# Cross-attention in a six-part decoder block: transposed scores on two 64-row groups, with the queries kept twice, in place of 17 rows on 32-row groups

## The reference, cut to what matters

```python
def _L0_xattn_ref(query, key, values, mask, W_out):
    q = query.reshape(N, Q, HEADS, HEAD_DIM)
    k = key.reshape(N, K, HEADS, HEAD_DIM)
    v = values.reshape(N, K, HEADS, HEAD_DIM)
    energy = jnp.einsum('nqhd,nkhd->nhqk', q, k)
    energy = jnp.where(mask == 0, jnp.float32(-1e+20), energy)
    attn = jax.nn.softmax(energy / jnp.sqrt(jnp.float32(EMB)), axis=-1)
    out = jnp.einsum('nhqk,nkhd->nqhd', attn, v).reshape(N, Q, EMB)
    return out @ W_out.T
...
    x = x + _L0_attn_ref(_layernorm(x, axis=-1), L0_attn_Wq, ...)
    x = x + _L0_xattn_ref(_layernorm(x, axis=-1), ctx_1024, ctx_1024, mask_Bx1x1xS2_ik0, L0_xattn_W_out)
    x = x + _L0_ffn_ref(_layernorm(x, axis=-1), ...)
    x = x + _L1_attn_ref(_layernorm(x, axis=-1), ...)
    x = x + _L1_xattn_ref(_layernorm(x, axis=-1), ctx_1024, ctx_1024, ...)
    x = x + _L1_ffn_ref(_layernorm(x, axis=-1), ...)
```

## Time and profile before

| | |
|---|---|
| median of 3 runs | 1816.44 us (1815.75 to 1816.7) |
| the profiled execution | 1815.63 us |
| its span, first to last instruction | 1813.8 us |
| PE busy | 1689.0 us (93%) |
| DVE, ACT, POOL busy | 777.8, 634.3, 441.8 us |
| mean granted TensorE clock | 0.846 of full speed |
| the chain that ended last | PE 85%, DVE 7% |
| L641 in that chain | 10% of the span |

### The profile page before, as it was taken

The page is one execution under the profiler, slowest core; times in us unless marked ns, Lnnn a source line. Parts: engine busy times, 40 slices in busy tenths (PEclk is TensorE's granted clock), DMA queues, the critical chain, the costliest instruction groups (busy, mean ns, idle before and its releaser), DMA issues.

```text
span 1813.8 us, 32813 instructions
## 1 busy us (share of the span) xinstructions
PE 1689.0 (93%) x11795; PEld 1158.1 (64%) x11795; DVE 777.8 (43%) x1752; ACT 634.3 (35%) x1684; POOL 441.8 (24%) x519
## 2 busy tenths in 40 slices
PE   5999999989999999987999799999998999699995
PEld 5888888757766766753555447565666666465653
DVE  4555555443333333314555412111204565456665
ACT  1221112112222223224666541312214666254552
POOL 2000000011101101008888410000003333345551
PEclk8999999955555555558999899999998999899996
DMA  6300000001110111040000010000000000000001
GB/s 181 54 1 0 0 0 0 1 19 28 36 37 19 36 37 27 1 153 1 1 0 0 1 44 0 1 0 0 0 0 6 1 0 1 6 9 10 8 6 41
DMA packets 33034, 34.72 MB, mean 19 GB/s; under 512 B 8913, under 2 KB 29633, under 8 KB 32945
## 3 DMA queue, kind: packets, MB, share of 16 engines
q1 hardware_dynamic: 32944, 33.48, 7.3%
HBM read 31.49 MB, written 1.86 MB: 18 GB/s over the span
## 4 chain that ended last, share of the span: by engine, by line
PE 85%; DVE 7%; issue 2%; ACT 2%; POOL 2%; DMA 1%; SPq 1%; DVEq 0%; ACTq 0%; POOLq 0%
PE banks L276 40%; PE banks L641 10%; PE banks L680 6%; PE banks L628 6%; PE banks L269 4%; PE banks L657 4%; PE banks L548 3%; PE banks L693 3%; PE banks L706 2%; PE banks L520 2%; PE banks L683 1%; DVE area L1427 1%; DMA room<-in_bo 1%; PE banks L869 1%; PE banks L715 1%
## 5 line engine op out<-in xcount | busy, mean ns | idle before, releaser
L1131 ACT ACTIVATE area<-banks,area 112x112 f32<-112x112 f32 x768 | 208.5, 360 | 147.0 <-DVE area L1427 135.4
L1395 DVE TENSOR_REDUCE Y_room<-banks 112x2 f32<-112x750 f32 x128 | 115.4, 936 | 244.3 <-PE banks L628 244.3
L680 PE MATMUL banks<-area 128*112 128x448 f32 x384 | 180.1, 551 | 6.9 <-POOL area L964 3.6
L1110 ACT ACTIVATE area<-banks,Y_room 125x896 f32<-125x896 f32 x96 | 96.7, 1007 | 231.1 <-PE banks L641 231.1
L269 PE MATMUL banks<-cst,area 112*128 112x112 f32 x576 | 102.0, 295 | 71.8 <-DVE area L1470 21.6
L1427 DVE TENSOR_REDUCE area<-banks 112x4 f32<-112x448 f32 x192 | 119.2, 621 | 93.0 <-PE banks L683 92.6
L255 POOL TENSOR_TENSOR rstd<-mv,kcol 112x1 f32<-112x1 f32 x80 | 15.2, 190 | 554.6 <-DVE mv L1265 515.2
L269 PEld LDWEIGHTS banks<-cst,area 112*128 112x128 f32 x576 | 64.2, 152 | 115.3 <-issue 83.9
L276 PE MATMUL banks<-area,room 128*128 128x112 f32 x1024 | 125.0, 286 | 5.8 <-DVE area L1292 3.6
L276 PEld LDWEIGHTS banks<-area,room 128*128 128x128 f32 x1024 | 122.9, 202 | 6.3 <-DVE area L1292 3.8
L693 PEld LDWEIGHTS banks<-cst,area 112*112 112x112 f32 x768 | 87.5, 133 | 55.6 <-issue 44.1
(11 more groups left out here) (214 smaller groups left out, 2905.3 us busy)
## 6 DMA issues: line engine op xcount, KB each, us to landing
Y_room<-in_ctx SPq DMA_DIRECT2D x16, 375.0 KB
area<-in_ctxT SPq DMA_DIRECT2D x64, 93.8 KB
l<-in_l SPq DMA_DIRECT2D x2, 1024.0 KB, 10.4
room<-in_ctxT SPq DMA_DIRECT2D x16, 112.0 KB, 2.1
out<-X SPq DMA_DIRECT2D x16, 112.0 KB, 1.9
X<-in_x SPq DMA_DIRECT2D x1, 1568.0 KB, 20.7
room<-in_Wq SPq DMA_DIRECT2D x1, 1024.0 KB, 7.6
room<-in_Wk SPq DMA_DIRECT2D x1, 1024.0 KB, 9.8
```

Of the source, the lines that this page charges most:

```text
L680: T3.matmul(pb[2 + g % 2][0:S, 0:4 * S], c_qT[u][:, k, :], c_kbd[u][:, k, j:j + 4, :].rearrange("p j s -> p (j s)"), start=True, stop=False)
L1110: a_.activation(b_pT[g][:, c, :, :], banks[0:KC, 4:6, 0:QN], ACT.Exp, bias=b_bias[v][:, c:c + 1]).then_inc(Bs["ex"].sem, 1)
L1131: last = a_.activation(c_p[:, h * S:(h + 1) * S], pb[2 + g % 2][0:S, j * S:(j + 1) * S], ACT.Exp, bias=c_nb[:, h:h + 1])
L1395: v_.tensor_reduce(b_nb[u][:, 8 * a + k:8 * a + k + 5:4], banks[0:S, 2 * a:2 * a + 2, 0:SC], AX_X, ALU.max, negate=True).then_inc(Bs["nb"] ...
```

## The change

`turned` contracts over 64 rows, two slots together, in place of 17 rows of one slot. Which head of the pair is meant is said by the queries: `b_q` is now kept twice (g = 0 and 1), and copy g has the rows of the other slot of each half zeroed. ACT makes the two copies from the same transposed bank, each with a column of scales that is 1/16 on one slot of each half and 0 on the other (a new constant, `C_HALF`). So that the two heads e that go together lie in different halves of the array, the heads' slots are ordered anew: slot r holds a = r % 2, c = r // 2, in `b_ctx`, in `b_xs` and in the columns of `b_nb`.

The mask row now lies within the 64 rows and has to be zero for `turned`. So `b_nb` has 32 columns, 16 of them zero (two memsets on POOL in the first stage), its transpose has 32 rows, and SP writes them with four DMAs: for each copy g the maxima into row 16 of its slots and zeros into row 17. `scores_b` still contracts over 18 rows of each slot, from the copy in which the slot is live. All four buffers of `b_q` move to `room`, where the first stage's weights were.

```diff
-C_END = C_LT + 16
+C_HALF = C_LT + 16
+C_END = C_HALF + 2
...
+    c[:, C_HALF:C_HALF + 2] = ((p[:, None] // SLOT) % 2 == np.arange(2)[None, :]) * D ** -0.5
...
-        b_q = [take(P, QN) for _ in range(2)]
+        b_q = [room[:, 2 * i * QN:2 * (i + 1) * QN].rearrange("p (g n) -> p g n", g=2) for i in range(4)]
...
-        b_nb, b_rc, b_nt = [beside_y(S, H) for _ in range(2)], beside_y(S, H), beside_y(H, S)
-        b_q = [beside_y(P, QN) for _ in range(2)] + b_q
+        b_nb, b_rc, b_nt = [beside_y(S, 2 * H) for _ in range(2)], beside_y(S, H), beside_y(2 * H, S)
...
-                    src = T["ctxT"][bass.ds(b, 1)].rearrange("o (a k c i) s -> a c (o i) k s", a=2, k=QUAD, c=2)[r // 2, r % 2]
+                    src = T["ctxT"][bass.ds(b, 1)].rearrange("o (a k c i) s -> a c (o i) k s", a=2, k=QUAD, c=2)[r % 2, r // 2]
...
-                    sp.dma_start(b_q[(w - 1) % 4][HD:P:SLOT, :].rearrange("r (k s) -> r k s", k=QUAD),
-                                 b_nt).then_inc(Bs["mr"].sem, 16)
+                    for n in range(4):
+                        first = SLOT * (n // 2) + HD + n % 2
+                        sp.dma_start(b_q[(w - 1) % 4][first:P:2 * SLOT, n // 2, :].rearrange("e (k s) -> e k s", k=QUAD),
+                                     b_nt[8 * n:8 * (n + 1), :]).then_inc(Bs["mr"].sem, 16)
...
-                    T3.transpose(pb[7][0:H, 0:S], b_nb[(w - 1) % 2], ident[0:S, 0:S]).then_inc(Bs["mt"].sem, 1)
+                    T3.transpose(pb[7][0:2 * H, 0:S], b_nb[(w - 1) % 2], ident[0:S, 0:S]).then_inc(Bs["mt"].sem, 1)
...
-                    last = T3.matmul(pb[r][0:S, 0:SC], b_q[w][o:o + HD + 2, k * S:(k + 1) * S], b_ctx[w][o:o + HD + 2, k, 0:SC],
+                    last = T3.matmul(pb[r][0:S, 0:SC], b_q[w][o:o + HD + 2, r % 2, k * S:(k + 1) * S], b_ctx[w][o:o + HD + 2, k, 0:SC],
...
-                        o = SLOT * (2 * g + e)
-                        last = T3.matmul(pb[4 + e][0:KC, k * S:(k + 1) * S], b_ctx[w][o:o + HD + 1, k, c * KC:(c + 1) * KC],
-                                         b_q[w][o:o + HD + 1, k * S:(k + 1) * S], start=True, stop=True)
+                        o = 2 * SLOT * e
+                        last = T3.matmul(pb[4 + e][0:KC, k * S:(k + 1) * S], b_ctx[w][o:o + 2 * SLOT, k, c * KC:(c + 1) * KC],
+                                         b_q[w][o:o + 2 * SLOT, g, k * S:(k + 1) * S], start=True, stop=True)
...
-                    a_.activation(b_q[(w + 1) % 4], pb[7][:, 0:QN], ACT.Copy, scale=D ** -0.5).then_inc(Bs["qs"].sem, 1)
+                    for g in range(2):
+                        last = a_.activation(b_q[(w + 1) % 4][:, g, :], pb[7][:, 0:QN], ACT.Copy,
+                                             scale=cst[:, C_HALF + g:C_HALF + g + 1])
+                    last.then_inc(Bs["qs"].sem, 1)
```

More of the change, by code:

```diff
@@ L635, in turned @@
                 if n == 0:
-                    pe.wait_ge(Bs["mr"].sem, Bs["mr"].at(16 * (b + 1)))
+                    pe.wait_ge(Bs["mr"].sem, Bs["mr"].at(64 * (b + 1)))
                 pe.wait_ge(Bs["ex"].sem, Bs["ex"].at(6 * b + n))
@@ L944, in phase_a @@
                     g_.memset(b_cv[1][:, :, :, HD:HD + 1], 1.0)
+                    for t in b_nb:
+                        g_.memset(t, 0.0)
                     g_.memset(b_xs[:, :], 0.0).then_inc(pre["bx"].sem, 1)
@@ L1076, in phase_b @@
                     act.wait_ge(Bs["mt"].sem, Bs["mt"].at(b))
-                    act.wait_ge(Bs["mr"].sem, Bs["mr"].at(16 * (b - 1)))
-                    a_.activation(b_nt, pb[7][0:H, 0:S], ACT.Copy).then_inc(Bs["me"].sem, 1)
+                    act.wait_ge(Bs["mr"].sem, Bs["mr"].at(64 * (b - 1)))
+                    a_.activation(b_nt, pb[7][0:2 * H, 0:S], ACT.Copy).then_inc(Bs["me"].sem, 1)
                 if on(b - 2):
@@ L1370, in phase_b @@
                     for a in range(2):
-                        dst = b_xs.rearrange("s (k a c e) -> s a k c e", k=QUAD, a=2, c=2)[:, a, :, :, 0:HD]
+                        dst = b_xs.rearrange("s (k c a e) -> s a k c e", k=QUAD, a=2, c=2)[:, a, :, :, 0:HD]
                         src = xb_(b + 1, a * P, (a + 1) * P).rearrange("s (k c e) -> s k c e", k=QUAD, c=2)
@@ L1394, in highest @@
                     dve.wait_ge(Bs["mt"].sem, Bs["mt"].at(b - 1))
-                v_.tensor_reduce(b_nb[u][:, 8 * a + k:8 * a + k + 5:4], banks[0:S, 2 * a:2 * a + 2, 0:SC], AX_X, ALU.max,
+                v_.tensor_reduce(b_nb[u][:, 4 * a + k:4 * a + k + H + 1:H], banks[0:S, 2 * a:2 * a + 2, 0:SC], AX_X, ALU.max,
                                  negate=True).then_inc(Bs["nb"].sem, 1)
```

## The result

The kernel takes **1653.2 us** with the change, the median of four runs (1651.6 to 1660.9), against 1816.3 before (1815.8 to 1816.7). The ratio is 0.911 (95% interval 0.909 to 0.913): 163 us less, where the forecast was 173 and its range 1612 to 1710.

A forecast was written before the change was run, and what follows sets the result against it. PE bound all stages, cross-attention at 1.2 GHz. A batch of 13.3 + 0.2 + 0.45 + 1.05 = 15.0 us, taken as 15.1 for 26.65, over 15.0 batches saves 173: 1816.4 - 173 = 1643 us; range 1612 to 1710.

The forecast's parts named there:

- The clock decides, and rows of zeros count: Cross-attention: addressed rows count, zeros included, so the clock rises from 0.50 and clock-scaled PE work falls from 26.65 to 13.3 us.
- The like case: L680 streams block-diagonal keys, 16 of 128 rows nonzero; four of those and one bf16 matmul at 0.50 preceded 0.97.
- It rises in the first batches with `turned`: Cross-attention: the clock rises in the first batches containing `turned`, which starts after 383 us; gain counted from 403 us.
- and to stay up: Cross-attention: once risen, the clock stays high to the stage's end at about 802 us, 15.0 batches' worth.
- Rival 2: Cross-attention: the clock goes up and down in stretches rich in L628 and small transposes; half the gain, 1730 us; chance 0.11.
- Rows do not make a matmul longer: `turned` in cross-attention: 64 rows at the higher clock take 65 ns per record, where 17 rows took 125 at 0.50.
- The small term beside it: `turned`: 2.5 ns per record above half of 125, over 96 records, 0.2 us per batch at the higher clock.
- Overlap lost, 0.45 us a batch: Three boundaries of `turned` and `scores_b` per batch: no free row groups, 0.9 us lost at 0.50, 0.45 at 1.00.
- Waits of fixed length, 1.05 us a batch: Cross-attention: PE waits for Exps (0.4 us at piece 5) and maxima (about 0.3), others 0.35; sum 1.05 us per batch.
- Cost at nothing: Second query copy on ACT, four maxima DMAs on SP, GpSimd's memsets, wider maxima transpose: hidden or off the path, no time.
- Rivals 1 and 3: Cross-attention: clock stays at 0.50, 1831 us, chance 0.12; or it rises but maxima, DMAs and Exps bind, 1686 us, 0.11.
- The sum: Cross-attention: 15.0 batches' worth, each falling from 26.65 to 15.1 us, give 173 us off 1816.4, so 1643 us.

The follow-up runs named there:

- The swap: Changed kernel with PE's loop written out, and the second scores (k = 1) moved ahead of piece 5 of `turned`: 1652.3 us, ratio 0.9089.

## Why the prediction was right, and where it was off

*The clock decides, and rows of zeros count*: right, and the experiments show it from both sides: rows taken away, and rows of zeros put in. The change with 17 rows stays at 0.50 and takes 1816.2 us. Rows of zeros alone, in the scores of the kernel before, bring it to 1676.9. The like case that the prediction argued from, block-diagonal keys ahead of a rise, pointed the right way (its four are records, so two matmuls). PE's busy time did not: it was busy in all of the 80.00 us above at 0.50, and in 33.65 of 40.60 us ahead of the rise. The rule of the Trainium skill, "TensorE: Matmul & The Clock Gate", Part 1, that keeping PE busy is enough for 2.4 GHz, does not hold in this kernel.

*It rises in the first batches with `turned`*: right, at 406.6 us; the prediction counted from 403. 3.6 us at the lower level, 3.6 x (1 - 15.1 / 26.65), are 1.6 us.

*"and to stay up"*: **this is the step that failed.** The prediction called PE never idle in the stage, read the batches of the kernel before as all alike, and had no row for the loop branch. There PE stalls for 2.74 us, and 23.9 us, from the end of the stall on, are at 0.50. The two batches concerned take 22.49 and 20.92 us in place of 15.19, 13.0 us more, of which some 2.7 are the stall and 10 the clock. That is the slowest run. Writing the loop out takes both away and brings 7 us by the medians, so in the usual run the dip costs less, about 4 us beside the stall (an estimate: 7 less the stall's 2.7 to 3.3; no such run has a trace). Rival 2, the clock up and down, was thus true for one dip, but for another reason than it gave, and in this run at about a ninth of its price (10 us of 87). In the batches of the changed kernel the small transposes and the scores did not let it fall.

*Rows do not make a matmul longer*: right. A piece of 16 records starts 451.91 to 452.97 = 1.06 us ahead of the next matmul, 66 ns a record; the prediction had 65. With 32 rows it is the same (594.38 - 593.32 = 1.06 at another piece of the version with 32 rows). The small term beside it was mis-sized: at 0.50 the same distance is 500.15 - 498.20 = 1.95 us, so 122 ns a record and not 125, and the higher clock leaves 5 ns above half of it, not 2.5. With six pieces of 16 records a batch that is 0.5 us in place of 0.2.

*Overlap lost, 0.45 us a batch*: 0.5 by the places, 15.19 - 14.66 = 0.53 by the batches. The Trainium skill's "TensorEngine Tiling (Array Packing)", Key Properties, has a drain at each change of tiling mode. Here the lost overlap at the three places accounts for the difference, so no further drain is to be seen, as the prediction took it.

*Waits of fixed length, 1.05 us a batch*: **the size came out by luck, the mechanism did not.** Without the 64-row groups a batch takes 14.66 us where halving gives 13.3, so 1.3 us don't scale with the clock, and the prediction had 0.2 + 1.05. But they are not waits. The weight loads of `turned` do wait 4.3 us for Exps in four batches, twelve times, three a batch, which looks like the 1.05; almost all of it passes while matmuls ahead still run, and PE's own idle time is 61.00 - 60.53 = 0.47 us in four batches. Nothing waits for the maxima in the steady batches. What is left over is spread over all groups of matmuls. `weighted` over 48 records, the kernel before at 0.50 (it starts at 491.59) and the changed kernel at 1.00:

```profile
493.96 1.81 PE L641 MATMUL banks<-Y_room,area 17*125 17x112 f32 x14
...
443.14 1.34 PE L660 MATMUL banks<-area 125*17 125x112 f32 x48
...
444.41 1.13 PE L644 MATMUL banks<-room,area 64*125 64x112 f32 x16
```

It takes 2.37 us and then 1.27, 0.085 more than half. The first scores go from 1.54 us to 0.83, 0.06 more than half. Each of the six pieces has 0.085, as above. Set side by side place by place, a batch of the kernel before (483.54 to 510.20) and one of the kernel before over 32 rows (447.18 to 461.86) differ from halving by 1.35 us, and only about 0.2 of it lies where a piece waits for an Exp, ahead of pieces 1 and 5 (an estimate from these starts). So the term that the prediction had too small is a fixed part of each group of matmuls, which it counted for `turned` alone, and the term too large is the waits. The swap fits: it removed the wait at piece 5 and gained nothing.

*Cost at nothing*: right at both clocks, for the second copy, the four DMAs and the memsets. At 0.50 the ratio is 1.0009, at 1.00 the batches of 14.66 and 14.67 us are equal with and without them. The four DMAs take 2.17 us of SP's queue (450.14 above), and PE waits for them only at the very first piece of the stage, 0.4 us.

*Rivals 1 and 3.* The clock did not stay low. Nor did waits take PE's place: PE is busy for 60.53 of 61.00 us, with VectorE at 36.72 / 4 = 9.2 us a batch and ScalarE at 8.3.

*The sum.* 173 us were expected of the stage, and it gave 152.0 between the two profiles; 2.7 more came behind it, which makes the 154.7. Of the 21.0 us missing, 13.0 are the stall and its dip, 15.0 x (15.19 - 15.1) = 1.4 the batch, 1.6 the rise; 5.0 are left for the first and last steps, which are not full batches. Against the medians the gain is 163.1: the other runs of the changed kernel are 7 to 9 us shorter than the profiled one, at a mean clock of 0.952 to 0.953 against 0.947, so their low stretches together must be shorter. Which one is, isn't shown, as they have no trace; a dip of the size seen with the scores over 32 rows would account for 7.1 us.

**Still open**: what exactly sets the moment of the rise and the fall. From one kernel to the next the rise in cross-attention came between 390.6 and 472.8 us. Widening the scores brought it earlier in all three pairs that differ by nothing else (406.6 to 390.6, 403.9 to 397.1, 418.5 to 397.9). But two kernels in which PE does the same until then differ by 19 us (433.6 and 414.1), so one trace each does not measure what a row is worth. With 32 rows in `turned` alone the four runs spread over 57 us, and only one of them has a trace. The low stretch at the stall does not follow the rows either: 30.7 us with both over 32 rows in the kernel before, 13.6 with the scores alone. None of these kernels was made to find the rule.

## What to carry to other kernels

Where PE is busy all the time and the granted clock still reads 0.50, look at how many rows its matmuls contract over, and first let them take in rows that hold zeros anyway: here two edited lines of the kernel before brought 152 of the change's 163 us. A stall can then cost more than its length (2.7 us of it, and 13.0 in all, in the profiled run), so look in the trace of before for idle time put down to "issue", at loop branches above all. And keep track of what shares the array: widening a matmul beyond its row group costs the overlap with its neighbours, here 0.5 us in 15. Last, a sum that comes out right does not prove its terms: here two wrong ones, the waits and the fixed part of each matmul, made up for each other.

## What the runs showed of the hardware

- Rows of zeros raised TensorE's clock from 1.2 to 2.4 GHz at no price in time: with 14 of them added to the scores alone, 1816 us became 1677, and eight records of scores take 0.83 us at the high clock over 18 rows as over 32.
- Stalls on PE at the loop branch came with stretches at the lower clock of very different length: 2.74 us with 23.9 (64-row pieces, 18-row scores), 3.27 with 6.9 (64 and 32), 3.22 with 20.5 (32 and 18), 2.75 with 30.7 (32 and 32), 2.99 with 13.6 (17 and 32). Neither the stall's length nor the rows put them in order.
- A PE program that loops back stalls there once, 2.0 to 3.3 us in the seven traces with the loop. Six of them show no semaphore to blame; the shortest, 1.99 us in the version with 17 rows, is put down to an Exp. Written out, the program does not stall.
- At twice the clock the fp32 matmuls of a batch took 1.35 us more than half of their time, spread over all of them: a piece of 16 records 1.95 and 1.06 us, 48 records of `weighted` 2.37 and 1.27.
